# Latent attention on one Trainium2 core: a pair's context products in one run, its output products spread over the three other slots

## What is computed

```python
xn, ln_lat = layer_norm(x, g1, b1), layer_norm(latents, g2, b2)   # latents: 64 tokens, x: 64 context tokens
q = ln_lat @ Wq
kv = jnp.concatenate([xn, ln_lat], axis=1) @ Wkv                  # 128 key tokens per sequence
weight = softmax(where(full_mask, q k^T / 8, -max))               # 16 heads of 64
out = (weight @ v).reshape(b, l, heads * dim_head) @ Wout
x = layernorm(latents + out)                                      # then the router of the expert layer
```

## Time and profile before

| what | value |
|---|---|
| median of 3 runs | 1788.88 us |
| the profiled execution's own time | 1788.39 us |
| its span, first to last instruction | 1786.7 us |
| TensorE busy (matmul records) | 1628.2 us, 91% |
| VectorE, ScalarE, GpSimd busy | 67%, 51%, 38% |
| latent attention, from its first query product to its last context products | 1139.4 to 1664.0 us |
| granted TensorE clock, 1180 to 1640 us | 1.00 |

### The profile page before, as it was taken

The page is one execution under the profiler, slowest core; times in us unless marked ns, Lnnn a source line. Parts: engine busy times, 40 slices in busy tenths (PEclk is TensorE's granted clock), DMA queues, the critical chain, the costliest instruction groups (busy, mean ns, idle before and its releaser), DMA issues. The chain is left out here.

```text
span 1786.7 us, 51780 instructions
## 1 busy us (share of the span) xinstructions
PE 1628.2 (91%) x18030; PEld 1354.3 (76%) x18030; DVE 1189.6 (67%) x3409; ACT 910.7 (51%) x2614; POOL 670.7 (38%) x1071
## 2 busy tenths in 40 slices
PE   6997799778899999999999997699999999999485
PEld 4775688667677777777777775599999999999354
DVE  4886588667466677766776676357777767776444
ACT  4775477533344544454545453365556556555131
POOL 2665365401133333333332333133444344434245
PEclk9999799889899999999999999799999999999798
DMA  1111512111101100110001000311111111111221
GB/s 51 46 43 33 172 54 58 37 39 56 26 22 30 30 24 24 28 31 24 24 25 32 26 24 22 85 54 48 49 58 58 48 48 58 58 51 45 71 83 50
DMA packets 156933, 82.28 MB, mean 46 GB/s; under 512 B 17561, under 2 KB 154059, under 8 KB 156464
## 3 DMA queue, kind: packets, MB, share of 16 engines
q1 hardware_dynamic: 149728, 71.35, 14.4%
q10 hardware_dynamic: 5072, 6.66, 1.1%
q0 software_dynamic: 2048, 3.15, 0.5%
HBM read 61.03 MB, written 21.27 MB: 46 GB/s over the span
## 5 line engine op out<-in xcount | busy, mean ns | idle before, releaser
L1135 PE MATMUL bank<-diff_xT,diff_w_score 128*128 128x128 f32 x2048 | 259.1, 280 | 0.8 <-ACT diff_xT L1239 0.8
L1135 PEld LDWEIGHTS bank<-diff_xT,diff_w_score 128*128 128x128 f32 x2048 | 241.7, 193 | 22.4 <-issue 20.6
L1246 ACT ACTIVATE diff_keys<-bank 128x512 f32<-128x512 f32 x256 | 152.4, 595 | 165.5 <-PE bank L1135 165.5
L1903 POOL TENSOR_TENSOR lat_prob<-lat_prob,lat_inv_sum 128x512 f32<-128x512 f32 x128 | 133.6, 1044 | 218.0 <-DVE lat_inv_sum L1816 202.5
L1429 POOL TENSOR_TENSOR diff_prob<-diff_prob,diff_inv_sum 128x512 f32<-128x512 f32 x64 | 67.2, 1050 | 379.7 <-DVE diff_inv_sum L1333 379.7
L1720 ACT ACTIVATE lat_prob<-bank,lat_neg_max 128x128 f32<-128x128 f32 x512 | 180.5, 372 | 1.0 <-DVE lat_neg_max L1838 1.0
L1731 ACT ACTIVATE lat_query<-bank 128x512 f32<-128x512 f32 x128 | 76.4, 597 | 175.6 <-PE bank L1614 175.6
L1644 PE MATMUL bank<-lat_catT,lat_query 128*128 128x128 f32 x1024 | 142.4, 282 | 3.9 <-ACT lat_query L1731 3.9
L1614 PE MATMUL bank<-lat_catT,lat_w_score 128*128 128x128 f32 x1024 | 139.7, 280 | 2.9 <-DVE lat_mask_bias L1877 0.8
L1644 PEld LDWEIGHTS bank<-lat_catT,lat_query 128*128 128x128 f32 x1024 | 125.2, 193 | 15.9 <-issue 10.6
L1614 PEld LDWEIGHTS bank<-lat_catT,lat_w_score 128*128 128x128 f32 x1024 | 126.0, 194 | 5.6 <-issue 4.0
(11 more groups left out here) (306 smaller groups left out, 3669.0 us busy)
## 6 DMA issues: line engine op xcount, KB each, us to landing
lat_c_rep<-cat SPq DMA_DIRECT2D x128, 128.0 KB
diff_x_rep<-stage SPq DMA_DIRECT2D x128, 32.0 KB, 1.7
lat_c_t<-cat SPq DMA_DIRECT2D x32, 128.0 KB, 2.1
exp_w<-in_L_ffn_w_dram SPq DMA_DIRECT2D x16, 256.0 KB, 3.4
expert_rows<-lat_zeros SPq DMA_DIRECT2D x4, 548.0 KB, 10.1
exp_rows<-expert_rows SPq DMA_DIRECT2D x8, 274.0 KB, 4.4
self_x_t<-in_x_dram SPq DMA_DIRECT2D x32, 64.0 KB, 1.8
self_x_res<-in_x_dram SPq DMA_DIRECT2D x32, 64.0 KB, 2.0
```

What stands on the lines that cost most here:

```text
L1135: last = nc.tensor.matmul(ring[(k + d) % 2][:, j * P:(j + 1) * P], w_score[:, H1 * (k // 2) + HS * d + 4 * (k % 2) + j, :], xT[:, :], star ...
L1246: nc.scalar.activation(keys[:, k // 2, 4 * (k % 2):4 * (k % 2) + 4, :].rearrange("p h t -> p (h t)"), ring[(k + d) % 2][:, :], ACT.Copy).t ...
L1903: nc.gpsimd.tensor_tensor(prob[:, q, :, :], prob[:, q, :, :], inv_sum[:, q, :, None].to_broadcast([P, 4, T]), ALU.mult)\
```

## The change

The contexts of both sequences of a pair run one after the other in slot 2. The 16 output products are numbered through (even heads 0 to 7, odd heads 8 to 15) and split into 5, 6 and 5: the first five of pair i-1 in slot 3, the next six in slot 0 and the last five in slot 1 of the pair that follows. The copies of the contexts out of PSUM move from slot 3 to slot 2, on ScalarE and on VectorE. The wait for the even banks now stands ahead of product 0, that for the odd banks ahead of product 8.

```diff
-            def outputs(i, odd):
-
-                for m in range(8):
+            def outputs(i, first, end):
+
+                for n in range(first, end):
+                    odd, m = n // (H1 // 2), n % (H1 // 2)
+                    if n == 0:
+                        wait(pe, even_copied, 2 * (i + 1))
+                    if n == (H1 // 2):
+                        wait(pe, odd_copied, 2 * (i + 1))
                     last = nc.tensor.matmul(ps_o, ctxT[:, 2 * m + odd, :, :].rearrange("p b s -> p (b s)"),
-                                            w_vo[:, odd, m, :], start=(odd == 0 and m == 0), stop=(odd == 1 and m == 7))
-                if odd:
+                                            w_vo[:, odd, m, :], start=n == 0, stop=n == H1 - 1)
+                if end == H1:
                     last.then_inc(o_done, 1)
...
                     if c == 0 and live(i - 2):
-                        pe.wait_ge(even_copied, 2 * (i - 1))
-                        outputs(i - 2, 0)
+                        outputs(i - 2, 5, 11)
                     if c == 1 and live(i - 2):
-                        pe.wait_ge(odd_copied, 2 * (i - 1))
-                        outputs(i - 2, 1)
+                        outputs(i - 2, 11, H1)
...
                         contexts(i - 1, 1 - par, 0)
+                        contexts(i - 1, 1 - par, 1)
                     if c == 3 and live(i - 1):
-                        contexts(i - 1, 1 - par, 1)
+                        outputs(i - 1, 0, 5)
...
-                    if c == 3 and live(i - 1):
+                    if c == 2 and live(i - 1):
 
                         act.wait_ge(c_done, i)
...
-                    if c == 3 and live(i - 1):
+                    if c == 2 and live(i - 1):
 
                         dve.wait_ge(c_done, i)
```

## The result

The changed kernel takes 1795.94 us, the median of 19 runs (1792.45 to 1802.45), against 1789.92 us of the kernel before in 19 runs (1786.06 to 1793.03): 1.0035 times, 95% interval 1.0026 to 1.0043, some 6 us slower. The profiled execution has a span of 1794.9 us against 1786.7.

The account below looks back on a forecast made before the run. TensorE was taken to set the phase's pace, with ScalarE's chain holding the shortened slot 3. Terms 2.7 + 0.7 + 1.3 gave +4.7 us, a forecast of 1793.3 us, range 1786.5 to 1798.

Parts of the forecast that it names:

- The merged run: Slot 2's joined contexts hold TensorE 3.67 us; with fewer switches and shorter transposes, 0.35 us saved a pair, -10.9 over 31.
- ScalarE's chain: Slot 3's query copy, exponentials and token copy: tokens ready 2.47 us after its middle work starts, 0.12 after TensorE wants them.
- The restart: TensorE's delay from token copy's end to next queries: 0.30 us, or 0.76 where the loop's branch follows.
- round ends: Pairs where the loop's branch precedes the next queries: 0.55 late less 0.35 saved, +0.20 us each, 13 times, 2.6.
- first halves: Pairs in a round's first half: queries 0.37 late less 0.35 saved, +0.02 us each, 13 times, 0.3.
- rival (b): At round ends the branch is cheap once the engine waits: queries 0.41 after the copy, 4.6 us less, 1788.7; 15%.
- Pairs 1, 2, 3, 30, 31: Pairs outside the regular loop: -0.4 us for 1 and 2, +0.2 for 3 and 30, +0.7 for 31.
- Moved copies, z, fourth transpose: Context copies in slot 2 stay covered, and z is ready 0.6 us before the contexts; cost 0.
- The end of the phase: After the last contexts, ranks, row choice and scatter come up to 1.45 us later, behind five output products; 1.3 taken.
- The sum: Periods of pairs 1 to 30 +2.7, pair 31 +0.7, phase end +1.3: +4.7 us in all.

Follow-up runs that it names:

- e1: Changed kernel with the token transposes moved ahead of slot 3's outputs and ScalarE's token copy ahead of its exponentials: 1778.5 us, 0.992 of the kernel before.
- e2: Kernel before, with transposes moved ahead of the second context run and the token copy ahead of slot 3's exponentials: 1787.72 us, 0.998 of the kernel before.
- e8: The changed kernel unaltered, run once more for its profile: 1796.04 us (one run).
- e3: Changed kernel with outputs split 6, 5, 5 over slots 3, 0, 1 instead of 5, 6, 5: 1789.14 us, 0.9985 of the kernel before.
- e4: Changed kernel with outputs split 7, 5, 4 over slots 3, 0, 1 instead of 5, 6, 5: 1787.46 us, 0.9974 of the kernel before.
- e5: e1 with pair 30's output products alone back in the old places, eight each in slots 0 and 1: 1776.29 us, 0.9922 of the kernel before.
- e6: e5 with, in pair 32 alone, the five output products behind slot 3's rank products: 1775.92 us, 0.9917 of the kernel before.
- e7: Changed kernel without the spreading: contexts merged in slot 2, outputs eight and eight in slots 0 and 1, only transposes in slot 3: 1829.08 us (one run).
- e9: Changed kernel with pair 30's output products alone back in the old places: 1795.25 us, 1.0041 times the kernel before.

## Why the prediction was right

It said slower, 1793.3 us, and 1786.5 to 1798; measured are 1795.94 and +6.0 us where +4.7 had been summed. Its steps in order:

**The merged run: right.** 3.66 us for 3.67, transposes 0.22 for 0.22. With nothing in the way (e1) a pair gains 16.08 - 15.70 = 0.38 us, for the 0.35 counted; against e2, which has the transposes in the same place, 16.11 - 15.70 = 0.41.

**ScalarE's chain: right.** Tokens ready at T + 2.47 in both halves, as worked out from pair 0's slot 3. What made this term possible was one place in the trace of before where the same instructions stood with nothing between them.

**The restart: right, each a little too large.** 0.26 us instead of 0.30 in the first half, 0.73 instead of 0.76 at round ends. So the first halves came out at -0.03 a pair for +0.02 and the round ends at +0.17 for +0.20, together 1.9 us for 2.9. The figure of the Trainium skill, Advanced Engine Details and Errata, Control Flow Timing (about 108 ns for a compare-and-branch), as the prediction's estimate used it, would have made the round ends 4.6 us cheaper. The trace has 0.207 us for the branch alone and 0.73 from copy to queries, and rival (b) falls with it.

**Pairs 1, 2, 3, 30, 31: right in sum, by luck.** I had -0.4, +0.2 and +0.7, in all +0.5. Measured are +1.0 up to pair 4 and -0.5 from pair 30 on. Two terms of the same size were left out, and they cancel. Pair 1 takes on five output products in its slot 3 and gives none away (+1.12): 0.94 measured, for 1.12 - 0.18. Pair 31 has five fewer in its slots 0 and 1 (-1.12): from its first queries to its contexts it takes 7.64 us instead of 8.76. What I did count there came as counted: from contexts to slot 3's mask it took 7.67 us instead of 6.97, +0.70.

**Moved copies, z, fourth transpose: right.** ScalarE's and VectorE's copies start with the end of the contexts, 1412.15 and 1412.07, and end at 1413.24 and 1413.36, ahead of T = 1413.93; no context run in the loop waits. z is ready 7.52 us after slot 3's mask and the contexts start 8.16 after it, so 0.64 us is to spare, for the 0.6 worked out.

**The end of the phase: mis-sized.** This is the step that failed: "ranks, row choice and scatter come up to 1.45 us later ... I take 1.3". Against the start of VectorE's copies the ranks came 1.3 later (2.53 us instead of 1.21), as taken, and the first load 0.9 later. What I had left out was the clock. With 11 instead of 16 products left for the last slots TensorE sat idle for 1.56 and 2.23 us ahead of the last contexts, where there were 1.07 and 1.56, and ran 3.4 us of that run at 1.2 GHz: +1.7 us in this profile, +2.7 in e8's. In all six profiles with the thinned last slots (the changed kernel's three, e1, e3 and e4) the run took 5.4 to 6.4 us; in all six with the full ones (before, e2, e5, e6, e7 and e9) 3.74.

The sum was close in part by luck: the loop's periods came out 1.0 us cheaper and the end 1.3 dearer (2.6 us for 1.3). Between the 5.0 us that the profiles account for and the measured 6 there is nothing left that the interval (4.7 to 7.7 us) could tell.

## What to carry to other kernels

When work is moved out of a slot, ask which chain on another engine that slot was long enough to hide: an engine that is busy for 59% of the time, like ScalarE here (153.6 of 260 us), sets a floor for one slot while its average says nothing. Look in the prologue for a place where that chain runs bare, and read its length there. And where a copy that feeds the next round stands last in its engine's program, try to put it first: here the same change, with the transposes moved ahead of the outputs and their copy ahead of the exponentials, turned 0.35% lost into 0.8% gained.

## What the runs showed of the hardware that I had not expected

A wait that stands in TensorE's own sequencer close to a loop's branch lets the branch show: 0.28 us a round in the kernel before, 3.19 - 2.73 = 0.46 us more at round ends than in first halves in the changed one, and 0.00 in e1 and e2, where the wait is met early and both halves last equally long. The branch's own record is 0.207 or 0.208 us long in all of these rounds, so its length alone does not say what it costs.

In the six profiles with the thinned last slots TensorE was idle for 1.56 to 1.71 us and then for 2.23 to 2.45 us ahead of the last contexts, and its clock stood at half for 3.4 or 6.8 us. In two of them it fell 0.8 to 0.9 us after these contexts had begun; in the other four it fell 1.4 to 2.1 us before them, early in the second idle time (read from the granted clock of stretches of 1 us). In the six others the idle times were 1.07 to 1.28 and 1.55 or 1.56 us, in four of these with 0.69 us more earlier, and the clock stayed whole through the last contexts. Thin slots are not the only thing that brings such a stretch: in e7 one came inside the loop, in pair 26 and in no other. A phase's last pairs can so cost more than their instructions, and an edit that leaves TensorE less to do there can lose by it.
